# Attention block on one core: probabilities transposed in 32x32 blocks by VectorE and regrouped by DMA, instead of transposed by TensorE

## The reference

```python
xn = layernorm(x)
# attention, 16 heads of 64
h  = (xn - mean) * rsqrt(var + eps) * ln_scale + ln_bias
c_q, c_kv = h @ w_down_q.T, h @ w_down_kv.T          # latents of 64
q, k, v = heads(c_q @ w_up_q.T), heads(c_kv @ w_up_k.T), heads(c_kv @ w_up_v.T)
q, k = rope(q), rope(k)    # pairs (e, o) -> (e*cos - o*sin, e*sin + o*cos)
attn = softmax(q @ k^T / 8)                          # 256 x 256 per head
attention = concat(attn @ v) @ w_out.T + xn
# ffn
y   = relu(xn @ W_fc.T) ** 2 @ W_proj.T              # 512 hidden
ffn = (number of spikes of 5 leaky integrate-and-fire steps driven by y) / 5
```

## Time and profile before

| | |
|---|---|
| median of 3 runs | 1274.29 us (1272.05 to 1274.43) |
| the profiled execution, its own time | 1276.49 us |
| its span in the trace | 1274.4 us |
| busy: TensorE / its weight loads | 1209.4 us (95%) / 942.4 us (74%) |
| busy: ScalarE | 1074.4 us (84%) |
| busy: VectorE | 954.2 us (75%) |
| busy: GpSimd | 806.8 us (63%) |
| DMA | 80.03 MB, mean 63 GB/s |

### The profile page before, as it was taken

The page is one execution under the profiler, slowest core; times in us unless marked ns, Lnnn a source line. Parts: engine busy times, 40 slices in busy tenths (PEclk is TensorE's granted clock), DMA queues, the critical chain, the costliest instruction groups (busy, mean ns, idle before and its releaser), DMA issues.

```text
span 1274.4 us, 33640 instructions
## 1 busy us (share of the span) xinstructions
PE 1209.4 (95%) x9952; PEld 942.4 (74%) x9952; DVE 954.2 (75%) x1734; ACT 1074.4 (84%) x3425; POOL 806.8 (63%) x773
## 2 busy tenths in 40 slices
PE   4899999999999999999999999999999999999997
PEld 3767777777777777777777777777777777777775
DVE  3677777877778777778777778777778777778774
ACT  1788888888888888898888888888988888988884
POOL 2766676656666666666656667566666666666561
PEclk9899999999999999999999999999999999999999
DMA  4111111111111111111111111111111111111110
GB/s 132 68 55 59 60 67 68 58 60 57 65 67 63 62 61 55 66 66 59 66 53 63 66 61 64 62 58 63 62 62 67 58 58 66 60 65 66 59 63 21
DMA packets 60065, 80.03 MB, mean 63 GB/s; under 512 B 9664, under 2 KB 26304, under 8 KB 59840
## 3 DMA queue, kind: packets, MB, share of 16 engines
q1 hardware_dynamic: 59968, 79.11, 17.4%
HBM read 7.77 MB, written 4.19 MB: 9 GB/s over the span
## 4 chain that ended last, share of the span: by engine, by line
PE 59%; issue 18%; DVE 9%; POOL 8%; ACT 4%; DMA 1%; DVEq 0%; ACTq 0%; POOLq 0%; SPq 0%
PE ps_t L305 12%; PE ps_u L319 12%; PE ps_s L295 12%; PE ps_b L395 6%; PE ps_a L363 3%; PE ps_a L353 3%; POOL qk_lo L751 3%; PE ps_qk L281 3%; ACT prob L490 3%; DVE cos_sin L604 3%; PE ps_qk L282 3%; POOL qk L745 2%; PE ps_b L387 2%; DVE latent L653 2%; DVE neg_max L613 2%
## 5 line engine op out<-in xcount | busy, mean ns | idle before, releaser
L490 ACT ACTIVATE prob<-ps_s,neg_max 128x256 f32<-128x256 f32 x1024 | 473.0, 477 | 106.3 <-DVE neg_max L613 80.3
L751 POOL TENSOR_TENSOR qk_lo<-qk,qk_hi 128x512 fp32r<-128x512 f32 x256 | 327.4, 1279 | 328.8 <-ACT qk_hi L498 328.7
L613 DVE TENSOR_REDUCE neg_max<-ps_s 128x2 f32<-128x512 f32 x512 | 329.8, 686 | 247.3 <-PE ps_s L295 246.4
L745 POOL TENSOR_TENSOR qk<-cos_sin,sin_sw 128x512 f32<-128x512 f32 x256 | 334.9, 1308 | 83.7 <-DMA sin_sw<-cos_sin 81.3
L604 DVE TENSOR_TENSOR cos_sin<-ps_qk,rope_sb 128x512 f32<-128x512 f32 x512 | 328.8, 683 | 18.0 <-PE ps_qk L282 15.6
L305 PE MATMUL ps_t<-ident_sb,prob 128*128 128x128 f32 x2048 | 279.7, 280 | 0.4 <-ACT prob_t L503 0.4
L503 ACT COPY prob_t<-ps_t 128x512 f32<-128x512 f32 x512 | 278.1, 610 | 0.0
L319 PE MATMUL ps_u<-prob_t,ckv 128*64 128x256 f32 x2048 | 277.6, 392 | 0.0
L305 PEld LDWEIGHTS ps_t<-ident_sb,prob 128*128 128x128 f32 x2048 | 222.1, 141 | 31.2 <-issue 1.0
L490 ACT ACTIVATION_READ_ACCUMULATOR prob<-ps_s,neg_max 128x1 f32 x1024 | 211.1, 206 | 0.0
L319 PEld LDWEIGHTS ps_u<-prob_t,ckv 128*64 128x64 f32 x2048 | 124.2, 136 | 97.9 <-issue 48.2
(11 more groups left out here) (64 smaller groups left out, 1440.9 us busy)
## 6 DMA issues: line engine op xcount, KB each, us to landing
sin_sw<-cos_sin SPq DMA_DIRECT2D x512, 128.0 KB, 2.1
x_sb<-in_x SPq DMA_DIRECT2D x32, 128.0 KB, 2.1
out<-out_sb SPq DMA_DIRECT2D x32, 128.0 KB, 2.0
wup_raw<-in_wup SPq DMA_DIRECT2D x2, 512.0 KB, 5.6
rope_sb<-in_rope SPq DMA_DIRECT2D x1, 512.0 KB, 6.6
wo_sb<-in_wo_t SPq DMA_DIRECT2D x1, 512.0 KB, 7.8
sel_raw<-in_sel SPq DMA_DIRECT2D x1, 512.0 KB, 8.6
wfc_sb<-in_wfc_t SPq DMA_DIRECT2D x1, 256.0 KB, 6.7
```

The source lines that it names most:

```text
L490: last = nc.scalar.activation(prob[:, s % 2, h, t, :], ps_s[h][:, t, :], ACT.Exp, bias=neg_max[:, s % 2, h, t:t + 1], accum_out=den[:, bpa ...
L613: nc.vector.tensor_reduce(neg_max[:, s % 2, h, :], ps_s[h][:, :, :], AXIS_X, ALU.max, negate=True).then_inc(max_ready[h], 1)
L745: nc.gpsimd.tensor_tensor(qk[:, s % 2, :, :], cos_sin[:, s % 2, 0, :, :], sin_sw[:, s % 2, :, :], ALU.add).then_inc(rope_done, 1)
L751: nc.gpsimd.tensor_tensor(qk_lo[:, s % 2, :, :], qk[:, s % 2, :, :], qk_hi[:, s % 2, :, :].bitcast(F32), ALU.subtract).then_inc(lo_ready, 1)
```

## The change

What it does, stage by stage:

- **Transposing.** TensorE's eight transposes and ScalarE's two copies of a pair go. VectorE's `turn` transposes each 32x32 block of `prob` in one instruction of 128x1024 elements (within a quarter of 32 partitions). Four pairs make a group; when a group is turned, `move` sends its blocks to the partitions where they belong: 16 DMAs of 128 KB (32 partitions x 4 KB), eight at the step of the group's last turn (`half` 0) and eight one step later (`half` 1). `weigh_latents` waits for all 16 at the first pair of a group (p = 0 and p = 4). `exponentials` writes `prob` in runs of 32 elements, and the matmul reads `gathered` in such runs.
- **Rotation.** VectorE multiplies by the cosine alone (one instruction, straight into `qk`); ScalarE copies `ps_qk` to SBUF (`copy_projected`); the copies of two pairs are exchanged together by two DMAs of 256 KB; GpSimd multiplies by the sine and then adds. `leading` and `rest` go.
- **Scores.** Plain float32: four matmuls (eight instructions) in place of twelve. The four banks won from `ps_s`/`ps_t` hold the scores of two pairs, so `row_max` is one instruction of 1024 elements for both heads, and `scores` waits for the exponentials of the pair two before.
- **Order.** The leads are now 11, 9, 7, 6, 0, and the once-a-batch work sits at other p; `drive` and `copy_y` go, so that `integrate` reads y from PSUM. `den`'s inverse is transposed into a spare half of `ps_u`. `square` works in place. Setup weights share memory with `turned`.

```diff
-LEAD = {"project": 5, "add": 4, "lead": 4, "rest": 3, "scores": 2, "transpose": 1, "multiply": 0}
+LEAD = {"project": 11, "rope": 9, "scores": 7, "turn": 6, "multiply": 0}
...
+            def exchange(g, s, i):
+                duo = s // 2
+                sp.wait_ge(raw_ready, done(g))
...
+                sp.wait_ge(rope_done, done(g - 4))
                 for odd in range(2):
+                    sp.dma_start(partner[1 - odd::2, duo % 2, :, :, :], raw[odd::2, duo % 2, :, :, :])\
+                        .then_inc(swapped[duo % 2], 16)
+            def move(g, s, half):
+                par = (s // GROUP) % 2
+                if half == 0:
+                    sp.wait_ge(turn_done, done(g))
...
+                    sp.wait_ge(u_ready, done(g - 2 * GROUP))
+                for rows in (2 * half, 2 * half + 1):
+                    for block_of in range(Q):
+                        sp.dma_start(gathered[32 * block_of:32 * block_of + 32, par, rows, :, :, :, :, :],
+                                     turned[32 * rows:32 * rows + 32, par, block_of, :, :]).then_inc(moved[par], 16)
@@ SP step
+                if (s + ahead) % 2 == 1 and not outside(g + ahead, STEPS):
+                    exchange(g + ahead, s + ahead, i)
+                if (s + turn) % GROUP == GROUP - 1 and not outside(g + turn, STEPS):
+                    move(g + turn, s + turn, 0)
+                if (s + turn) % GROUP == 0 and not outside(g + turn - 1, STEPS):
+                    move(g + turn - 1, s + turn - 1, 1)
@@ PE
-                pe.wait_ge(rot_ready, done(g - 1))
+                pe.wait_ge(raw_ready, done(g - 1))
...
+                        last = nc.tensor.matmul(ps_s[:, s % 2, h, t, :], qk[rows, s % 4, 0, t * P:(t + 1) * P],
+                                                qk[rows, s % 4, 1, :], start=True, stop=True)
...
+                if s % GROUP == 0:
+                    pe.wait_ge(moved[(s // GROUP) % 2], (i * (BODY // GROUP // 2) + s // GROUP // 2 + 1) * 16 * Q * Q)
...
+                pe.wait_ge(u_evac, done(PAIRS * b + 3))
@@ PE extras(b, b0, p), n = b + 1
                     elif p in (1, 2):
                         ffn_in(n, p - 1)
+                    elif p == 6:
+                        ffn_out(n, 1)
...
-                    if p == 5:
+                    if p == 3:
                         transpose_inputs(b + 2, b0)
-                    elif p == 6:
+                    elif p == 4:
                         latents(b + 2)
...
+                    if p == 0:
+                        broadcast_rden(b - 1, 3)
+                    elif p < 5:
+                        attention_out(b - 1, p - 1)
+                    elif p == 5:
+                        transpose_sum(b - 1)
+                if p >= 5 and not outside(b, B):
+                    broadcast_rden(b, p - 5)
@@ PE step: scores, transpose_rden (p == 4), extras, project, ffn_out(b + 1, 0) (p == 5), weigh_latents
@@ ACT step: copy_rden (p == 4), exponentials, then
                     elif p in (1, 2):
                         relu(n, p - 1)
...
+                    if p == 2:
+                        normalise(b + 2, b0, 0)
+                        normalise(b + 2, b0, 1)
+                    elif p == 3:
                         copy_inputs(b + 2)
+                if not outside(g + LEAD["project"], STEPS):
+                    copy_projected(g + LEAD["project"], s + LEAD["project"], i)
                 if not outside(g, STEPS):
                     copy_u(g, s, i)
@@ DVE
+                nc.vector.tensor_tensor(qk[:, s % 4, :, :], ps_qk[:, :, :], cos_sb, ALU.mult).then_inc(cos_ready, 1)
...
+                nc.vector.transpose(turned[:, par, :, s % GROUP, :],
+                                    prob[:, s % 2, :, :, :, :, :].rearrange("p j h k t c -> p j (h k t c)"))\
+                    .then_inc(turn_done, 1)
@@ DVE step: add_spikes (p == 5), row_max, invert_sums (p == 1), finish (p == 5), turn, rotate, then
+                if p == 0:
...
+                        normalise_u(b - 1, 3)
...
+                        moments_of(b + 2, b0, i + 1)
...
+                elif p == 4 and not outside(b + 2, B):
                     split_latents(b + 2, b0)
+                elif p >= 5:
                     if not outside(b, B):
+                        normalise_u(b, p - 5)
+                    if p >= 6 and not outside(b + 1, B):
+                        for k in ((0, 1), (2, 3, 4))[p - 6]:
+                            integrate(b + 1, 1 - b0, k)
@@ POOL add_rotated
+                other = partner[:, duo % 2, s % 2, :, :]
+                nc.gpsimd.tensor_tensor(other, other, sin_sb, ALU.mult).then_inc(sin_ready, 1)
...
+                nc.gpsimd.tensor_tensor(qk[:, s % 4, :, :], qk[:, s % 4, :, :], other, ALU.add).then_inc(rope_done, 1)
```

## The result

The kernel after takes 1412.01 us (median of 4 runs, 1409.66 to 1415.83) against 1274.20 us before: 1.109 times as long, interval 1.106 to 1.112. The forecast was 1242 us, faster.

The account below looks back on a forecast made before the run. It took TensorE to bound the kernel before; afterwards waits between engines, chiefly the move detour, set the period: 30 + 31.9 x 37.0 + 33 = 1242 us. Forecast's own range 1205 to 1285; 8 in 10: 1150 to 1335.

Parts of the forecast that it names:

- The frame: Whole span: first row maximum at 30 us, 31.9 batches times the period of 37.0 us, tail of 33 us.
- The transposing: VectorE's transposing instruction: 1.20 us, one source streamed by elements, like a row maximum over 1024 elements.
- Its rival of 2.4 us: VectorE's transposing fills a block before draining it, without overlap: 2.4 us an instruction, 1459 us in all; chance 0.09.
- so faster moves alone win about 1 us here: VectorE's steps p = 2 to p = 5: a second path through TensorE ends at 14.2 us, against 15.2 through the moves.
- the moves just hidden: Leg from VectorE's p = 6 to next p = 1: moves path 13.0 us, VectorE's own work 13.2, so 13.2.
- the detour's size: SP's exchange and move issues behind the raw copy: 0.547 us an issue, 2.1 us landing, 7.1 us from copy to landed.
- the leg from T2 to T5: From start of VectorE's step p = 2 to that of p = 5: 15.2 us, through raw copy, SP's issues, product and scores.
- The failed step: full clock: TensorE's work on the path was priced at full clock, clock 1.00, in the 37.0 us period.
- T5 to T6: VectorE 3.9, TensorE [...] 3.9: 4.0: Leg from VectorE's step p = 5 to p = 6: both engines need 3.9 us, the leg 4.0.
- Clock: Rival: TensorE idles and its clock falls to 0.9, adding about 2.5 us a batch; period 39.5, 1322 us; chance 0.10.
- Shared paths: Rival: moves of a half share half of the paths, rate 178 GB/s; period 40.6, 1357 us; chance 0.07.
- Nothing overlapped fully: Rival that everything overlaps: the period falls to VectorE's 32.1 us a batch, 1087 us; chance 0.12.

Follow-up runs that it names:

- e1: Changed kernel with SP issuing the second half of the moves ahead of the exchange: 1379.91 us, 1.082 times the kernel before.
- e3: Changed kernel plus float32 matmuls with overwritten results where TensorE would idle (before latents by token and products of p = 0, p = 4): 1330.02 us, 1.042.
- e2: Changed kernel with the exchange's two DMAs issued by ScalarE right behind its raw copy instead of by SP: 1356.11 us, 1.063.
- e17: e11 plus two TensorE matmuls with overwritten results ahead of the latents by token, after copy_u: 1304.98 us, 1.023 times the kernel before.
- e4: Changed kernel with each half of the moves reading both sides of 64 partitions instead of one: 1396.34 us, 1.095.
- e11: Changed kernel with exchange on ScalarE behind copy_u, turn and rotate ahead of invert_sums, move halves reading both sides; no added matmuls: 1364.79 us, 1.071.
- e18: e17 with the output's matmuls ahead of the transposes of the inputs (p = 3) and of the latents (p = 4): 1325.09 us, 1.039.
- e13: Changed kernel with scores and turn one step ahead (leads 8 and 7 in place of 7 and 6): 1609.78 us, 1.266.
- e7: e3 with 8 moves of 256 KB in place of 16 of 128 KB, blocks misplaced so the output is not kept: 1342.37 us, 1.053.
- e9: e7 with each half of the moves reading both sides of 64 partitions, blocks still misplaced: 1329.99 us, 1.043.

## Why the prediction was wrong, by its own steps

- **The frame, right.** First row maximum 29.9 (30), tail 33.2 (33), 31.9 periods between.
- **The transposing, right.** 1.234 us an instruction, 1.16 from start to start (1.20). The reason given, one source streamed element by element, fits: the row maximum over as many elements takes 1.222. The Trainium skill says in "Vector Engine (DVE) Microarchitecture Reference", section "3.8 The reshape front-end and per-opcode configuration", that the transposing mode is pipelined and sustains one element per cycle and lane. The trace agrees: 1234 ns for 1024 elements. Its rival of 2.4 us is out.
- **Small terms.** Row maximum 1.13 start to start (1.15), rotation 0.57 to 0.65 (0.60), exponentials 476 ns, as before; float32 scores 1.06 to 1.09 at full clock (1.01); thresholds 1.24 for three, 0.41 each (0.34).
- **The failed step: "so faster moves alone win about 1 us here" and "the moves just hidden"; the detour's size.** Its path was right: SP waits for the raw copy, the moves queue behind the exchange, the product of p = 4 waits. Its size was not: 0.635 us an issue for 0.547 and 2.44 us of landing for 2.1, since moves follow each other closely where the exchange's issues of the earlier trace rows stood in pairs: in the changed kernel's chain the first issue of a pair takes 0.51 us and each one behind it about 0.6. 8.2 for 7.1 us, twice a batch, is 2.1 us. At p = 0 the moves passed from hidden to late by it. e1, which takes the moves' wait away, shortens the leg from T2 to T5 by 1.9 us.
- **The failed step: full clock.** The fall stood as a rival (0.10, period 39.5), the forecast had TensorE's work on the path at full clock. Over 24 batches the product-to-product times at p = 0 and p = 4 are 2.11 and 0.37 us above those of e3, 2.5 us a batch, and e3 gains 2.6 in time with its own cost in it. The batch shown above has 1.45 and 0.78 of it.
- **The failed step: "T5 to T6: VectorE 3.9, TensorE [...] 3.9: 4.0".** The two engines do not run side by side in this leg: `ffn_out` waits for `finish`, behind the row maximum. The leg is 4.86 or 4.87 us on average in e1, e2, e3 and e17, 0.9 us more, and 4.93 in the changed kernel.
- **The sum.** 2.1 for the detour, 2.5 for the clock and 0.9 for `finish` are 5.5 of the 5.6 us by which the average legs (42.3) exceed the forecast ones (36.7). Clock and detour are not wholly apart, since it is the wait for the moves that leaves TensorE idle.
- **Missed altogether:** TensorE's 2.33 us wait for VectorE's thresholds at p = 0. In time alone it costs nothing here, because the product behind it waits for the moves until 709.6 anyway; filling it is what ends the half clock in e17.
- **The rivals.** Clock: right in mechanism and in its size for itself (2.5 forecast; 2.5 read over 24 batches, at least 2.6 by e3), too small alone. Shared paths: there is such a limit, 205 to 213 GB/s from one side against 239 from both, but not the 178 forecast, and behind issues of nearly the same rate; e4 gains 1.1% by taking it away. Float32 scores pair up. Nothing overlapped fully: VectorE's own 32 us never were the period.
- **Open.** Why e17, with the clock mended, has a period of 38.95 us ((1271.4 - 30.0)/31.875) and not the 36 to 37 of my legs. 0.9 of it is the leg from T5 to T6. For the rest its chain passes the normalisations, ScalarE's exchange issues and 16 moves on SP, but no run took these apart. What decides whether the clock falls is open too, as the last section shows. Nor was y copied out of PSUM again, nor a queue for the moves on another engine tried.

## What to carry to other kernels

Moving work off the engine that bounds a kernel makes it wait for others, and here a TensorE that idled between its stages paid again at half clock in the stages behind: look at the granted clock behind each idle stretch, and not only at the busy share. Read more than one batch: the clock fell at p = 4 in the batch shown and in six others of 24. A detour over DMA costs its issues one by one on one queue, and whoever shares the queue is late by all of them; before a step is moved, look at what stands behind it. When two limits are nearly equal, an experiment that lifts one shows little, and one that lifts both shows its worth only where nothing else covers the wait.

## What the runs showed of the hardware

- Before each half clock named here TensorE had idled, but the length of a single stretch does not tell it. Half clock followed idle stretches of 2.33 and 1.39 us (changed kernel), 2.32 and 0.98 us (e11), 1.91 us (e18), 2.96 us (e13, before the scores at 736.22), and in most batches 1.35 and 1.17 us (e2). It did not follow 1.46 us and then 0.75 to 1.75 us with 2.3 us of work between them (e17), nor 2.2 to 2.6 us at p = 4 in 17 of 24 batches of the changed kernel. TensorE was busy 81% of the span there, at a mean clock of 0.91.
- Adding work made the kernel faster: 2 matmuls a batch, 60 us (e11 to e17).
- DMAs of 128 KB were issued every 0.635 us when queued, of 256 KB every 0.8 us (3.20 for four). The rate of SBUF-to-SBUF moves was 205 to 213 GB/s from 64 partitions of one side (e7) and 239 GB/s when DMAs in one queue took turns between the sides (e9).
